# A five-layer attention kernel: key pieces moved from VectorE to GpSimd, three normalisations' scale and shift split between ScalarE and GpSimd, constants filled elsewhere, and a new order of steps

## The chip, the cores and the metric

The kernel runs on one core of a Trainium2 chip. A core has five engines, each working through its own instructions in order: TensorE (PE in the profile; its weight loads are PEld), VectorE (DVE), ScalarE (ACT), GpSimd (POOL) and SyncE (SP, which issues all DMAs here). They wait for one another by semaphores. The metric is the device time of one execution in microseconds.

## The reference

For each of 16 independent batch entries, x and a context of 256 tokens by 256 features go through five attention layers of 16 heads of 16 features each:

- `self` and `cross`: per head a 16 by 16 projection of keys, queries and values, masked softmax(QK/16), an output projection, a residual and a layer norm with gain and shift (ln1, ln2). `cross` is followed by a ReLU MLP of 1024 hidden features with its residual and norm (ln3).
- `l1`: a second norm of the queries (g_q, b_q), projections with bias, attention over the normalised context, output projection and residual.
- `l2`: windowed attention (64 tokens to either side) with a single key and value head, a gate (SiLU of a projection of the attention's output and the queries), an RMS norm, and the subtraction of the mean over tokens.
- `l3`: a norm, attention over the normalised context, residual, a norm, and a GELU MLP with its residual; its result is stored.

The keys of `self` and `cross` are the features of x and of the context themselves, since the key projection is folded into that of the queries.

## The kernel before, in words

**Work and stages.** Every batch entry is one chain of steps (CHAIN: some 40 steps for each layer) and one short chain beside it (BESIDE: loads, masks, the context's norm, the keys of the later layers). A tile has 128 partitions; 256 tokens or features are two such halves. Up to three batches are under way at once, each in its slot of buffers (SLOTS = 3).

**One attention layer on the engines.** `q` (PE, L1058 or L1293) projects. `ksplit` and `qsplit` cut keys and queries into three bfloat16 pieces each: the high piece by ScalarE (`high`, L697 to L712), the rest and the two lower pieces by VectorE (`low`, L841 to L866), then SP places them by six DMAs in a stack of 96 rows (L510), so that one bfloat16 matmul of 96 rows gives a nearly float32 product. `max0` to `max7` (PE L1096 and L1100, DVE L943) compute the scores of two heads each and their negated maxima. `pieces0`, `pieces1` (POOL, L664 and L667) cut the maxima of four such steps into three bfloat16 pieces, `turn0`, `turn1` (PE L1231, ACT L733, SP L523) turn them into three further rows of the query stack, against rows of ones in the key stack. `exp0` to `exp7` (PE L1118 to L1126, ACT L726) compute the scores again, less the maxima, and exponentiate; `weigh` (L1148 to L1157) multiplies by the values; `out`, `mix`, `outT` and `proj` normalise, turn and project. There are two score buffers and two `work` banks in PSUM.

**Norms.** `ln` (DVE, `moments`, L797 and L800) takes mean and variance, POOL makes the reciprocal root (L591 to L595), and `lnb` finishes on DVE. Where gain and shift are vectors (`self.ln`, `cross.ln`, `cross.ln3`, `cross.lnq`), it is done in two parts: `scale` (L816, subtract the mean, times the gain) while POOL works, and `shift` (L824, times the reciprocal root, plus the shift). `lnT` and `lnqT` transpose on PE (L1049), ScalarE takes the turned tile (`take`, L681), and POOL adds the next bias to the untransposed one for the next residual (`with_bias`, L605).

**Start.** VectorE fills values, PSUM and, at L787, rows 96 to 127 of the three key stacks with ones, and then lets PE, POOL and others go by the semaphore `zeroed`. Setup steps (`fold`, `columns_l1`, `row_l1` and so on) fold weights and biases once, among the first batches' steps.

**What sets the order.** Nothing is decided at run time. ORDER is a string of 3461 letters, written out by hand or by a program, each naming the chain whose next step comes: 0 to f the main chain of a batch, A to P the one beside it, s the setup. All engines walk through this one list, and each does its own part of every step; so ORDER, CHAIN, BESIDE and SETUP_STEPS fix the order of work in every queue, SP's too. Numbers count how often a semaphore must have been raised.

Of the kernel before, what the change touches and what calls it, by code (L numbers as in the profile page):

```python
# [8 lines left out]
ALU = mybir.AluOpType  # L9
# [31 lines left out]
     ("l3_b1", FC)],  # L41
# [26 lines left out]
for _name in BIAS_SOURCES:  # L68
# [19 lines left out]
    "self.mix0 self.values self.mix1 self.outT self.proj self.ln self.lnb self.lnT cross.q cross.qsplit cross.max0 "  # L88
# [3 lines left out]
    "cross.outT cross.proj cross.ln cross.lnb cross.lnT cross.hid1 cross.hid2 cross.hid3 cross.hid0 cross.hid_out "  # L92
# [22 lines left out]
def beside_steps():  # L115
# [7 lines left out]
ORDER = (  # L123
    "As0sAAsAAssA0001ssAssAA00A00sA2B00As01BB0B01B001s0000B000BA01B100001B10001010B0C11101C10C0C101B11110"
    "1C0011111221s100s01020000CsC00s100s0B2B10010s021221101C0C02s0021212200120002202022011022010212011100"
    "0012C110C001202C0211221AA10112001C21s112211001010200211102102011120010221000101D2211220222102100210B"
    "012B02200012D22122112C2C2002201122211021101111000212111112211202112111011012110020120120001211020012"
    "1022200110A210DA0011012101010021111D0101021212211021212121E200222002112212220202202BB202102012212200"
    "20200020202000110C0C000010221200s1001002002E0122220211202202002222222D1221010221121021101D1201321231"
    "1123322103112111112312312333131333312233133331313221D3DD3213D2E32D212E23321123E01242341322E2344E2EE3"  # L130
    "232232244E22E424423444F42E224D432444D43431424242444424E4332432334F3233F44332453343334433543343G342F3"
    "F343343344334F44443434F44454353DD4244F43444544F5F535354345355F545345555354534335543453453F5454555533"
    "4555345334353335F5435345E5344333343355E33353455353535554455355F55F5355355345434544354444534354454344"
    "4545543554433D5D4445444343343534335H34554333445435443534433354533E3544433E54454434434435544545535534"
    "43534544544443543534354435553345555G54554453553453443353353444443444445G34444444H3444444343443433345"
    "33343353335433345435345G54354443355G5355GG5353357566455565565555GG555565G665H666565466H676H576567366"
    "6656666H55677567777FH57F7776657H5777H7775G66H67767H77675I555777577755G755H375576575H57557675555556G5"
    "555577657777I57777766I57777H577I667H5776I75II655776I67I66I6766775876676676686676886I7675767766I76788"
    "666868686687768686778866878676886778G888688887678G678768677777768788J76778756767876867667867678777I8"
# [1300 lines left out]
```

## Time and profile before

| | us |
|---|---|
| median of 3 runs (lowest to highest) | 2636.02 (2631.29 to 2638.97) |
| profiled execution | 2635.18 |
| its span | 2633.4 |
| PE busy, 18862 matmuls | 2410.2 (92%) |
| DVE busy | 1590.7 (60%) |
| ACT busy | 1121.1 (43%) |
| POOL busy | 542.3 (21%) |

The span runs from the first to the last instruction; what lies around it is 1.8 us. Busy PE time is not PE at its peak: matmuls overlap, and the column of a group's mean is from a matmul's start to its modelled end. What a matmul really adds is seen where many follow one another in the chain of waits.

### The profile page before, as it was taken

How to read it: one execution, taken by the hardware profiler on the slowest of the kernel's cores; microseconds unless marked ns; L12 is line 12 of the kernel's file. 1: busy time of each engine (PE TensorE's matmuls, PEld its weight loads, DVE VectorE, ACT ScalarE, POOL GpSimd, SP SyncE). 2: the span in 40 equal slices, each digit the busy share in tenths (PEclk: the TensorE clock that was granted, in tenths of full speed). 3: DMA queues.
4: the chain of work that ended last, by engine and by line, in shares of the span. 5: the costliest groups of instructions: out<-in, count | busy, mean ns of one | idle time of the engine just before them, and what ended most of it. 6: DMA issues, size and time to landing. Idle time of an engine off the chain costs nothing.

```text
span 2633.4 us, 49701 instructions
## 1 busy us (share of the span) xinstructions
PE 2410.2 (92%) x18862; PEld 1749.2 (66%) x18862; DVE 1590.7 (60%) x2676; ACT 1121.1 (43%) x1762; POOL 542.3 (21%) x1278
## 2 busy tenths in 40 slices
PE   6999989999998898999989899999999999998976
PEld 4676766667676675766757567676767676676654
DVE  7756566665656557466574754766665757567432
ACT  1344345453444434535344344444444534544422
POOL 3221112222212132221112321111222212212110
PEclk8999999999999899999999999999999999999986
DMA  6412122231221122212111221211322221121100
GB/s 214 115 50 56 34 56 78 58 88 49 62 54 42 38 78 75 66 38 58 45 54 50 79 79 42 62 42 42 83 67 77 61 60 38 38 79 38 37 21 17
DMA packets 164235, 159.15 MB, mean 60 GB/s; under 512 B 17824, under 2 KB 162720, under 8 KB 162976
## 3 DMA queue, kind: packets, MB, share of 16 engines
q1 hardware_dynamic: 164000, 155.97, 21.6%
q8 instruction: 153, 2.51, 0.4%
q14 instruction: 82, 0.67, 0.1%
HBM read 35.71 MB, written 4.19 MB: 15 GB/s over the span
## 4 chain that ended last, share of the span: by engine, by line
PE 56%; issue 22%; DVE 8%; ACT 4%; POOL 3%; POOLq 2%; DVEq 2%; DMA 1%; SPq 1%; ACTq 0%
PE work L1067 13%; PE work L1058 11%; PE out L1148 6%; PE unit L1126 6%; PE unit L1100 5%; DVE neg_max L943 4%; PE unit L1096 4%; PE unit L1122 3%; ACT probs L726 2%; PE work L1049 2%; PE work L1263 2%; POOLq L669 1%; POOL resid L605 1%; DMA query_stack<-max_rows 1%; POOLq L666 1%
## 5 line engine op out<-in xcount | busy, mean ns | idle before, releaser
L943 DVE TENSOR_REDUCE neg_max<-unit 128x4 f32<-128x1024 f32 (+1 forms) x640 | 728.8, 1165 | 335.3 <-PE unit L1100 328.9
L726 ACT ACTIVATE probs<-unit 128x1024 f32<-128x1024 f32 (+1 forms) x640 | 609.1, 980 | 527.6 <-PE unit L1126 525.5
L1067 PE MATMUL work<-par,hidden_t 128*128 128x256 f32 x1792 | 417.9, 383 | 9.4 <-ACT hidden_t L681 6.0
L1100 PE MATMUL unit<-key_stack,query_stack 96*128 96x256 bf16 x2048 | 356.4, 280 | 35.4 <-DVE neg_max L943 17.9
L1067 PEld LDWEIGHTS work<-par,hidden_t 128*128 128x128 f32 x1792 | 332.4, 190 | 63.1 <-ACT hidden_t L681 9.7
L1126 PE MATMUL unit<-query_stack,key_stack 99*128 99x256 bf16 x2048 | 350.0, 277 | 25.6 <-ACT probs L726 9.2
L1058 PE MATMUL work<-tok_t,par 128*128 128x256 f32 x1408 | 339.0, 389 | 7.6 <-ACT tok_t L681 5.1
L1100 PEld LDWEIGHTS unit<-key_stack,query_stack 96*128 96x128 bf16 x2048 | 193.6, 100 | 162.4 <-DVE neg_max L943 38.6
L1058 PEld LDWEIGHTS work<-tok_t,par 128*128 128x128 f32 x1408 | 262.3, 194 | 49.6 <-ACT tok_t L681 9.9
L1148 PE MATMUL out<-probs,values 128*17 128x256 f32 x4096 | 269.6, 383 | 2.1 <-ACT probs L726 1.9
L1126 PEld LDWEIGHTS unit<-query_stack,key_stack 99*128 99x128 bf16 x2048 | 193.4, 99 | 90.0 <-ACT probs L726 19.4
L664 POOL CAST max_pieces<-neg_max 128x16 bf16<-128x16 f32 x160 | 34.0, 212 | 896.9 <-DVE neg_max L943 896.5
L757 ACT ACTIVATE hidden_t<-work,par 128x256 f32<-128x256 f32 x256 | 107.3, 470 | 191.3 <-PE work L1058 191.2
L1148 PEld LDWEIGHTS out<-probs,values 128*17 128x17 f32 x4096 | 95.6, 97 | 107.9 <-issue 48.3
L733 ACT CAST max_rows<-work 24x256 bf16<-24x256 f32 x160 | 57.0, 356 | 200.0 <-PE work L1231 199.6
L593 POOL TENSOR_SCALAR var_eps<-mv 128x2 f32<-128x2 f32 x112 | 25.4, 227 | 528.1 <-DVE mv L800 526.0
L681 ACT COPY tok_t<-work 128x512 f32<-128x512 f32 x96 | 56.1, 585 | 148.6 <-PE work L1049 148.2
L829 DVE TENSOR_TENSOR summed<-work,resid 128x512 f32<-128x512 f32 x64 | 44.2, 691 | 122.2 <-PE work L1067 121.9
L1263 PE MATMUL work<-ident,hidden_t 128*128 128x128 f32 x640 | 98.7, 282 | 15.6 <-ACT hidden_t L740 10.8
L1096 PE MATMUL unit<-neg_cross,ident_b 128*128 128x512 bf16 x256 | 97.6, 381 | 10.8 <-DVE neg_max L943 6.4
L963 DVE TENSOR_TENSOR hidden_t<-work,recip 128x256 f32<-128x256 f32 x160 | 99.5, 622 | 12.6 <-issue 0.9
L961 DVE RECIPROCAL recip<-work 128x16 f32<-128x16 f32 x160 | 40.0, 250 | 109.2 <-PE work L1263 108.6
(162 smaller groups left out, 3408.7 us busy)
## 6 DMA issues: line engine op xcount, KB each, us to landing
query_stack<-query_pieces SPq DMA_DIRECT2D x480, 128.0 KB, 2.4
key_stack<-key_pieces SPq DMA_DIRECT2D x384, 128.0 KB, 2.4
c_in<-in_ctx SPq DMA_DIRECT2D x16, 256.0 KB, 2.9
tok_t<-in_x_features SPq DMA_DIRECT2D x16, 256.0 KB, 2.8
ctx_t<-in_ctx_features SPq DMA_DIRECT2D x16, 256.0 KB, 3.0
x_in<-in_x SPq DMA_DIRECT2D x16, 256.0 KB, 3.1
m_in<-in_mask_self SPq DMA_DIRECT2D x16, 256.0 KB, 3.4
par<-in_params SPq DMA_DIRECT2D x4, 1024.0 KB, 6.3
```

Of the source, the lines that this page charges most:

```text
L726: a_.activation(probs[:, n % PROB_BUFS, :, :, 0:width(l)], bank[:, :, :, 0:width(l)], ACT.Exp, scale=SCALE[l]).then_inc(exped, 1)
L757: last = a_.activation(hidden_buffer(b, l)[:, f, :], bank[:, k, :], func, bias=pv(bias)[:, f:f + 1])
L943: v.tensor_reduce(neg_max[:, n % HALVES, :, 2 * (u % 4):2 * (u % 4) + 2], bank[:, :, :, 0:width(l)], AX.X, ALU.max, negate=True).then_inc( ...
L963: v.tensor_tensor(out_tok(b, l)[:, t, :].rearrange("p (c d h) -> p h c d", c=C, h=HC), slots[:, :, 0:HD].rearrange("p (h c) d -> p h c d", ...
L1058: last = pe.matmul(bank[:, k, :], pv(weight, C)[:, c, column + k * P:column + (k + 1) * P], src[:, c, :], start=(c == 0), stop=(c == C - 1))
L1067: last = pe.matmul(bank[:, t, :], src[:, t * P:(t + 1) * P], weight, start=(n == 0), stop=(n == len(parts) - 1))
L1096: pe.matmul(bank[:, t, :, 0:n], ident_b[:], twice(masked[:, t, 0:n], n), start=True, stop=False)
L1100: last = pe.matmul(bank[:, t, i, 0:n], queries[0:ROWS, h, t * P:(t + 1) * P], keys[0:ROWS, 0 if l == "l2" else h, columns(l, t)], start=ma ...
L1122: pe.matmul(bank[:, k, :, t * P:(t + 1) * P], masked[:, t, k * P:(k + 1) * P], twice(ident_b[:], P), start=(t == 0), stop=False)
L1126: last = pe.matmul(bank[:, k, i, 0:n], keys[0:MAX_ROWS, 0 if l == "l2" else h, k * P:(k + 1) * P], queries[0:MAX_ROWS, h, columns(l, k)], ...
L1148: last = pe.matmul(dst, values[b % SLOTS][:, k, head_in(NJ * g + j), :], p, start=(k == 0), stop=(k == T - 1))
L1263: last = pe.transpose(flatten(bank[:])[:, g * P:(g + 1) * P], out_t(b, l)[:, g, t * P:(t + 1) * P], ident[:])
```

## The change

Seven things change.

1. The low key pieces are made by POOL (`low_keys`). For `self` and `cross` POOL makes all of rest, second and third piece; for `l1`, `l2` and `l3` VectorE still makes the rest out of PSUM, which POOL can't read.
2. In `self.lnT`, `cross.lnT` and `cross.lnqT` VectorE gives the plain normalised tile (`layer_norm`); ScalarE puts gain and shift on the turned one, by one activation per half with a column of gains and one of shifts, and POOL multiplies the untransposed one by the gain. The shift is added once, at setup, to the bias that POOL adds anyway.
3. The ones of key stack 1 are written by ScalarE, of stacks 0 and 2 by POOL, with semaphores of their own, for which PE waits at the first `exp0` on each stack.
4. The third piece of the maxima is written by the subtraction itself, without a cast: four operations in place of five.
5. The hidden buffer of `self` and of `cross` comes free at another point (`wait_hidden_free`).
6. Six columns are added to the packed parameters.
7. CHAIN, BESIDE, SETUP_STEPS and ORDER are new. In `self`, `cross`, `l1` and `l3` `pieces0` follows four max steps, where it followed five in most layers before; the loads of batch 0 and 1 come first; `columns_l1` and `columns_l3` come later.

```diff
 BESIDE = (
-    "self.loadc self.loadct self.loadx self.loadm self.ctxln self.inputs self.loadm2 l2.keys l2.ksplit self.negc "
+    "self.loadc self.loadct self.loadx self.loadm self.inputs self.ctxln self.loadm2 l2.keys l2.ksplit self.negc "
 SETUP_STEPS = (
-    "par0 fold par5 par1 par7 wo_self wo_cross turn_wo columns_l1 par6 par4 columns_l3 par2 row_l1 row_l3 row_l2 "
-    "turn_bo par3 bg wg par8 "
+    "par1 par0 fold wo_cross wo_self par5 turn_wo par7 par8 par2 par6 par4 columns_l3 row_l2 columns_l1 par3 row_l1 "
+    "turn_bo bg wg row_l3 "
 ORDER = (
-    "As0sAAsAAssA0001ssAssAA00A00sA2B00As01BB0B01B001s0000B000BA01B100001B10001010B0C11101C10C0C101B11110"
+    "0AABAs1sAs000A1ABsAAs00s0A00000A00sBB0100B0s100BB0AB0s0B000110110001s10sA0sB01110B10112110A11100100s"
...
+            def ones_in_stack(n):
+                g.drain()
+                g.memset(key_stack[n][ROWS:P, :, :], 1.0).then_inc(stack_ones[n], 1)
+                g.drain()
+
+            ones_in_stack(0)
+            ones_in_stack(2)
             pool.wait_ge(setup_loaded, 48)
             pool.wait_ge(zeroed, 1)
...
+            def low_keys(key):
+
+                b, l, _ = key
+                part = (slice(0, HD), slice(0, 1)) if l == "l2" else (slice(0, P), slice(0, C))
+                piece = [key_pieces[part[0], n, part[1], :] for n in range(3)]
+                rest = key_rest[part[0], part[1], :]
+                if l in ("self", "cross"):
+                    pool.wait_ge(key_high, KSPLIT_NO.upto(key))
+                    g.tensor_tensor(rest, (tok_t[b % SLOTS] if l == "self" else ctx_t[b % CONTEXTS])[:], piece[0], ALU.subtract)
+                    g.drain()
+                else:
+                    wait_taken(pool, (b, l, "keys"))
+                g.tensor_copy(piece[1], rest).then_inc(key_low, 1)
+                g.drain()
+                g.tensor_tensor(piece[2], rest, piece[1], ALU.subtract).then_inc(key_low, 1)
...
+                    elif (l, step) in AFFINE:
+                        gain, _, bias = AFFINE[l, step]
                         wait_full_work(pool, key)
...
+                        g.tensor_tensor(resid[s][:], resid[s][:], row(gain), ALU.mult)
+                        g.drain()
+                        with_bias(resid[s], resid[s], bias)
...
-                        for piece in range(3):
-                            src = neg_max[:, half] if piece == 0 else max_rest[:]
-                            last = g.tensor_copy(max_pieces[:, n % HALVES, :, HC * piece:HC * (piece + 1)], src)
-                            if piece < 2:
-                                g.drain()
-                                g.tensor_tensor(max_rest[:], src, max_pieces[:, n % HALVES, :, HC * piece:HC * (piece + 1)],
-                                                ALU.subtract)
-                                g.drain()
-                        last.then_inc(max_cut, 1)
+                        piece = [max_pieces[:, n % HALVES, :, HC * k:HC * (k + 1)] for k in range(3)]
+                        g.tensor_copy(piece[0], neg_max[:, half])
+                        g.drain()
+                        g.tensor_tensor(max_rest[:], neg_max[:, half], piece[0], ALU.subtract)
+                        g.drain()
+                        g.tensor_copy(piece[1], max_rest[:])
+                        g.drain()
+                        g.tensor_tensor(piece[2], max_rest[:], piece[1], ALU.subtract).then_inc(max_cut, 1)
+                        g.drain()
...
         def _(act):
+            act.wait_ge(zeroed, 1)
+            a_.copy(key_stack[1][ROWS:P, :, :], ones[ROWS:P, 0:1].unsqueeze(2).broadcast_to((P - ROWS, H, S))).then_inc(stack_ones[1], 1)
...
-                    elif step in ("lnT", "lnqT"):
+                    elif (l, step) in AFFINE:
+                        gain, shift, _ = AFFINE[l, step]
+                        bank, taken = wait_full_work(act, key)
+                        wait_loaded(act, b, gain + "c", shift + "c")
+                        for c in range(C):
+                            last = a_.activation(tok_t[s][:, c, :], bank[:, c, :], ACT.Identity,
+                                                 scale=pv(gain + "c")[:, c:c + 1], bias=pv(shift + "c")[:, c:c + 1])
+                        last.then_inc(taken, 1)
+                    elif step == "lnT":
                         take(key, tok_t[s][:])
...
             v.memset(ones, 1.0)
-            for s in range(KEY_STACKS):
-                v.memset(key_stack[s][ROWS:P, :, :], 1.0)
...
-                        if l in ("self", "cross"):
-                            scale(scaled(b, l), summed[s], key)
-                    elif step == "lnb" and l in ("self", "cross"):
-                        shift(resid[s], scaled(b, l), (b, l, "ln"))
                     elif step == "lnb":
-                        layer_norm(norm[s], (resid if l == "l3" else summed)[s], (b, l, "ln"))
+                        layer_norm((resid if l in ("self", "cross") else norm)[s], (resid if l == "l3" else summed)[s],
+                                   (b, l, "ln"))
...
+                if u == 0 and l != "l2" and KEY_NO.place[b, l, "ksplit"] < KEY_STACKS:
+                    pe.wait_ge(stack_ones[KEY_NO.place[b, l, "ksplit"]], 1)
```

## Rows read from the trace of the kernel before

**Rows 1.** The page's first part: busy us, share, instructions of each engine.
```profile
PE 2410.2 (92%) x18862; PEld 1749.2 (66%) x18862; DVE 1590.7 (60%) x2676; ACT 1121.1 (43%) x1762; POOL 542.3 (21%) x1278
```

**Rows 2.** Busy time by stretch (count); then granted clock, DMA share, GB/s.
```profile
0.00:60.00 60.00, 38.18 (x182) 27.14 (x183) 44.87 (x78) 7.14 (x11) 19.25 (x37) 0.84 0.74 230
60.00:2500.00 2440.00, 2278.21 (x18118) 1657.04 (x18116) 1508.21 (x2533) 1079.51 (x1696) 510.72 (x1210) 0.99 0.22 59
2500.00:2634.00 134.00, 93.80 (x564) 65.06 (x564) 37.62 (x66) 34.40 (x57) 12.33 (x32) 0.80 0.07 19
```

**Rows 3.** Waits of TensorE, whole span: us in total, times, longest.
```profile
PE work L1168 <- DVEq L788: 19.0, 1, 19.0
PE unit L1100 <- DVE neg_max L943: 17.9, 32, 3.0
PE work L1231 <- POOL max_pieces L664: 17.8, 19, 2.5
```

**Rows 4.** The chain that ended last, in time: start, us, what.
```profile
70.24 0.22 PE unit L1126 x2
...
588.90 6.93 PE work L1067 x32
```

**Rows 5.** Timeline of the start: start, us, engine line operation.
```profile
4.29 0.20 POOL L583 MEMSET mean_w<- 128x128 f32 x1
...
6.78 3.47 DVE L787 MEMSET key_stack<- 32x4096 bf16 x1 [0.89 <-issue]
...
33.53 0.59 PE L1096 MATMUL unit<-neg_self,ident_b 128*128 128x512 bf16 x1
```

**Rows 6.** ScalarE, groups by form: busy us, mean ns, idle before.
```profile
L757 ACT ACTIVATE hidden_t<-work,par 128x256 f32<-128x256 f32 x256 | 107.3, 470 | 191.3 <-PE work L1058 191.2
...
L681 ACT COPY tok_t<-work 128x512 f32<-128x512 f32 x96 | 56.1, 585 | 148.6 <-PE work L1049 148.2
```

**Rows 7.** GpSimd, groups by form: busy us, mean ns, idle before.
```profile
L664 POOL CAST max_pieces<-max_rest 128x16 bf16<-128x16 f32 x320 | 73.0, 228 | 43.5 <-issue 2.4
L605 POOL TENSOR_TENSOR resid<-resid,par 128x512 f32<-128x512 f32 x48 | 56.3, 1172 | 128.1 <-PE work L1049 128.1
```

**Rows 8.** Timeline of the last batch's l3 attention, columns as in rows 5.
```profile
2564.52 3.78 PE L1058 MATMUL work<-tok_t,par 128*128 128x256 f32 x8 [0.68 <-ACT tok_t L681]
...
2569.31 3.81 SPq L510 DMA_DIRECT2D query_stack<-query_pieces  x6
...
2575.01 1.86 PE L1100 MATMUL unit<-key_stack,query_stack 96*128 96x256 bf16 x8 [6.71 <-issue]
...
2583.02 0.42 PE L1231 MATMUL work<-ident_b,max_pieces 128*128 128x128 bf16 x2
...
2586.10 1.03 PE L1126 MATMUL unit<-query_stack,key_stack 99*128 99x256 bf16 x4 [1.74 <-DMA query_stack<-max_rows]
```

**Rows 9.** VectorE by line (shortest/median/longest ns), then groups by form (busy us, mean ns).
```profile
L943 DVE TENSOR_REDUCE neg_max<-unit x640: 925/1215/1226, 35.7 to 2584.4; 128x4 f32<-128x1024 f32 x127, 128x4 f32<-128x768 f32 x33
...
L866 DVE TENSOR_TENSOR key_pieces<-key_rest,key_pieces x80: 411/693/1553, 23.1 to 2490.4; 128x512 bf16<-128x512 f32 x64, 16x256 bf16<-16x256 f32 x16
...
L864 DVE CAST key_pieces<-key_rest x80: 280/427/1543, 22.6 to 2489.9; 128x512 bf16<-128x512 f32 x64, 16x256 bf16<-16x256 f32 x16
...
L808 DVE TENSOR_SCALAR norm<-c_in,mv,rstd x32: 384/408/419, 40.6 to 2353.9; 128x256 f32<-128x256 f32 x32
...
L824 DVE SCALAR_TENSOR_TENSOR resid<-hidden_t,rstd,par 128x256 f32<-128x256 f32 x96 | 45.0, 510 | 5.3 <-POOL rstd L595 5.3
L816 DVE SCALAR_TENSOR_TENSOR hidden_t<-summed,mv,par 128x256 f32<-128x256 f32 x96 | 43.4, 493 | 4.4
```

**Rows 10.** Timeline at 841 us.
```profile
841.73 1.26 POOL L643 TENSOR_TENSOR hidden_t<-hidden_t,summed 128x512 f32<-128x512 f32 x1
...
841.80 1.66 DVE L808 TENSOR_SCALAR norm<-summed,mv,rstd 128x256 f32<-128x256 f32 x2 [2.14 <-POOL rstd L595]
```

**Rows 11.** Busy time of one stretch, columns as in rows 2.
```profile
865.00:880.00 15.00, 14.01 (x55) 7.94 (x54) 12.92 (x12) 1.31 (x3) 2.66 (x13) 0.50 0.12 36
```

More of the change, by code:

```diff
@@ L177 @@
 BIASES = (("self", "inputs"), ("self", "lnT"), ("cross", "lnT"), ("cross", "lnqT"), ("l2", "mean"), ("l3", "proj"))
-GAIN = {("self", "ln"): ("ln1_g", "ln1_b"), ("cross", "ln"): ("ln2_g", "ln2_b"), ("cross", "ln3"): ("ln3_g", "ln3_b"),
-        ("cross", "lnq"): ("g_q", "b_q")}
+AFFINE = {("self", "lnT"): ("ln1_g", "ln1_b", "bo_cross"), ("cross", "lnT"): ("ln2_g", "ln2_b", "l0_b2"),
+          ("cross", "lnqT"): ("g_q", "b_q", "bo_l1")}
 class Numbers:
@@ L361, in build @@
         zeroed = sem("zeroed")
+        stack_ones = [sem(f"stack_ones{s}") for s in range(KEY_STACKS)]
         band_ready = sem("band_ready")
@@ L433, in wait_hidden_free @@
             b, l = before
-            if l in ("self", "cross"):
-                act.wait_ge(normed, T * NORMED_NO.upto((b, l, "lnb" if l == "self" else "lnqb")))
-            elif l == "l1":
+            if l == "cross":
+                act.wait_ge(normed, T * NORMED_NO.upto((b, l, "ln3b")))
+            elif l in ("self", "l1"):
                 wait_full_work(act, (b, l, "proj"))
@@ L629, in run @@
                         negative(neg["cross"][s], 2 * b + 2)
+                    elif step == "ksplit":
+                        low_keys(key)
                     elif step == "values":
@@ L834, in low @@
                 of_keys = step == "ksplit"
-                pieces, done, ready, no = ((key_pieces, key_low, key_high, KSPLIT_NO) if of_keys
-                                           else (query_pieces, query_low, query_high, QSPLIT_NO))
-                rest = key_rest if of_keys else query_rest
+                if of_keys and l in ("self", "cross"):
+                    return
+                pieces, ready, no, rest = ((key_pieces, key_high, KSPLIT_NO, key_rest) if of_keys
+                                           else (query_pieces, query_high, QSPLIT_NO, query_rest))
@@ new lines, in low @@
+                bank, taken = wait_full_work(dve, (b, l, "keys" if of_keys else "q"))
+                if l in ("self", "cross"):
+                    last = v.tensor_tensor(rest[:], bank[:], pieces[:, 0], ALU.subtract)
+                elif of_keys and l == "l2":
+                    wait_loaded(dve, b, "bk_l2")
+                    v.tensor_copy(values_l2[b % SLOTS][:, :, 0:HD],
+                                  bank[:, 1, 0:T * HD].rearrange("p (t d) -> p t d", t=T))
+                    last = v.scalar_tensor_tensor(
+                        out=rest[0:HD, 0, :], in0=bank[0:HD, 0, :], scalar=pv("bk_l2")[0:HD, :],
+                        in1=pieces[0:HD, 0, 0, :], op0=ALU.add, op1=ALU.subtract)
+                else:
+                    wait_loaded(dve, b, "bk_" + l, "bq_" + l)
+                    bias = pv(("bk_" if of_keys else "bq_") + l)
+                    for c in range(C):
+                        last = v.scalar_tensor_tensor(
+                            out=rest[:, c, :], in0=bank[:, c, :], scalar=bias[:, c:c + 1],
+                            in1=pieces[:, 0, c, :], op0=ALU.add, op1=ALU.subtract)
@@ L862, in low @@
+                last.then_inc(taken, 1)
+                if of_keys:
+                    return
                 v.drain()
-                part = (slice(0, HD), slice(0, 1)) if of_keys and l == "l2" else (slice(0, P), slice(0, C))
-                v.tensor_copy(pieces[part[0], 1, part[1], :], rest[part[0], part[1], :]).then_inc(done, 1)
+                v.tensor_copy(query_pieces[:, 1], rest[:]).then_inc(query_low, 1)
                 v.drain()
-                v.tensor_tensor(pieces[part[0], 2, part[1], :], rest[part[0], part[1], :],
-                                pieces[part[0], 1, part[1], :], ALU.subtract).then_inc(done, 1)
+                v.tensor_tensor(query_pieces[:, 2], rest[:], query_pieces[:, 1], ALU.subtract).then_inc(query_low, 1)
@@ L917, in setup_step @@
                     last = v.tensor_tensor(pv(name), bank[:, 0, :], pv(name), ALU.add)
+                    if step == "row_l1":
+                        wait_loaded(dve, B, "b_q")
+                        v.drain()
+                        v.tensor_tensor(pv(name), pv("b_q"), pv(name), ALU.add)
                 elif step == "turn_bo":
@@ L994, in run @@
                         moments(norm[s], key)
-                        scale(scaled(b, l), norm[s], key)
                     elif step == "lnqb":
-                        shift(resid[s], scaled(b, l), (b, l, "lnq"))
+                        layer_norm(resid[s], norm[s], (b, l, "lnq"))
                     elif step == "hid_out":
```

116 lines of the change are left out of this document (50 added, 66 removed), and 33 rows, old and new, of the table CHAIN.

## The prediction

> **What bounds the kernel now.** I read the page first, then the busy time by stretch, the waits of TensorE, the groups of each other engine, and last the timeline of the start and the end. The page has TensorE (PE) busy for 92% of the span, VectorE (DVE) 60%, ScalarE (ACT) 43%, GpSimd (POOL) 21% [rows 1]. So no side engine is the bound on average; they matter where PE, which works through its list in order, has to wait for one. The three stretches of [rows 2] show where: PE idles 60.0 - 38.2 = 21.8 us in the first 60, 2440 - 2278.2 = 161.8 us in the 2440 of the middle (6.6%), and 134 - 93.8 = 40.2 us in the last 134, where only batches 14 and 15 are left and the clock is 0.80. Together 224 us. In the middle no single wait is long: the largest names are the maxima on DVE (17.9 us) and the pieces of maxima on POOL (17.8 us); the one long wait, 19.0 us, is the first matmul's [rows 3].
>
> How much could go at all? I weighed each step of ORDER by its TensorE time: 6.93/32 = 0.217 us for a float32 matmul of 256 columns, half of that for a bfloat16 one [rows 4], so 1.73 us for a projection, 6.93 for hid_out, 0.43 or 0.87 for a max or exp step without or with mask, 0.66 for l2's, 0.98 for a weigh. The steps are the same before and after and add up to about 2309 us. The span is 324 us above that: idle time, stretches at half clock, and waits too short to leave PE idle. That is the room.
>
> **The change, part by part.** The sum is made against the profiled execution's 2635.2 us (span 2633.4), 0.8 us under the median of the runs.
>
> *Start.* DVE fills three key stacks before it lets PE go: 3.47 us each with 0.8 between, so the first matmul is at 19.0 [rows 3]. Without them DVE is done at about 6.8, where the first of the fills began [rows 5]. ScalarE then makes one stack (a copy of 4096 elements a lane: at the 585 ns of its copies of 512 at most 4.7 us [rows 6], beside the loading of batch 0) and POOL two (no such row; DVE's 3.47 is the lower bound, and POOL's 228 ns for 16 elements and 1172 for 512 [rows 7] give 1.9 ns each, 7.8 us, the upper; I take 4, near DVE's row). But what PE needs for its first max is both stacks, and POOL now cuts the low key pieces after its two fills: its constants end at 4.5 [rows 5], so it is free at about 4.5 + 8 = 13 and done with three operations at 16.5. In the SP queue the six DMAs of the queries then take 3.8 us to issue, and at the end of the trace the first max follows 1.9 us behind the last of them [rows 8]. With the loads in the same queue that puts the first max near 23 to 25, not at 33.5 [rows 5]. That is 9 us earlier, but PE used the gap before for setup matmuls which now come later, in the dense part (some 3 us), and between the first maxima and the first exp there is then nothing to fill with. I take -6 (0 to -12). If POOL's fills took 7.8 each, the first max would be at 32 and the term 0.
>
> *DVE.* Gone are the key pieces, 64 x 0.427 + 16 x 0.28 = 32 us of casts and 64 x 0.693 + 16 x 0.41 = 51 of subtractions; the first subtraction in self and cross, 32 x 0.69 = 22; the fills, 10; `scale` of three norms (two thirds of 43.4, and 32 x 0.49 for lnq: 45) and the 45.0 us of `shift` into resid [rows 9]. Added: 96 plain normalisations at 0.41, 39 us. Net 32 + 51 + 22 + 10 + 45 + 45 - 39 = 166 us, so DVE falls to about 1425. What DVE has queued ahead of a maximum gets shorter by a tenth; of the waits of PE for it (17.9 us under the largest name alone [rows 3]) perhaps that share goes, and a little more where two waits meet: -5 (0 to -15).
>
> *POOL.* Added: 32 key splits of subtraction, cast, subtraction and 48 of the last two, 48 multiplications by the gain. A 512-element operation with two inputs is 1.17 us [rows 7]; a cast of 512 has no row, between 0.6 (half of that row) and 1.2; I take 0.8. So 32 x 3.2 + 32 x 2.0 + 16 x 1.1 + 48 x 1.17 + 8 for the fills = 248 us. One operation fewer in each of 160 pieces: -36 (0.228 x 160) [rows 7]. Net +212: 542 becomes about 750, 28%. The pieces of maxima now stand behind up to 3.2 us of a key split, and POOL, not DVE, waits for ScalarE's high piece and for DVE's rest. The cover is the PE work between the last max of a half and its turn (5.3 us on average in the new order, 6.0 in the old). Below nothing too: the pieces themselves end 0.35 us sooner, which stands in the counts below. I take +4 (0 to +25).
>
> *ScalarE.* Three transposes a batch are evicted by two activations of 470 ns instead of one copy of 585 [rows 6]: +0.36 us on the way lnT to q or hid, 48 times. Other batches' steps cover most; +3 (0 to +10).
>
> *New order.* Here I count, in PE work by the weights above, what ORDER places between a step and the one that needs it, and what falls short of the delay in between. The delays, from the end of the trace, where nothing else is in the way [rows 8]: q's end (2568.3) to first max 6.7 us; turn to exp 3.1; last maximum to turn: a reduction of 1.2 and five small POOL operations of 0.34 with their gaps, 2.9 (2.55 with four); exp to weigh 1.4, an estimate from ScalarE's 585 ns for half of its elements [rows 6]. Shortfalls, old to new order: turn to exp 30.3 to 19.1 us; q to max0 28.9 to 15.6; last max to turn 17.4 to 12.1; exp to weigh 10.1 to 2.8; four max steps in a row quicker than DVE's 1.22 each [rows 9], 21.4 to 11.8; gate to mean 12.5 to 7.6; the mix, outT, proj chain 51 to 50; proj to lnT 66 to 67; lnT to its reader 15.6 to 13. Sum 253 to 199. The middle's real idle time of 162 us is 0.64 of 253, and delays overlap once one has stalled; I take half of the difference of 54: -27 (0 to -50).
>
> *End.* The last batch's own chain (its l2 out to the store) is the same list with l3's keys put behind the rms, where PE has nothing of another batch; the small pieces come 0.35 us sooner in each half. -3 (+3 to -8).
>
> Sum: -6 - 5 + 4 + 3 - 27 - 3 = -34, so 2635.2 - 34 = 2601, and with the 0.8 us to the median 2602.
>
> **A row on the shared port.** At 841.73 a POOL subtraction of 1.26 us began, and DVE's pair of normalisations begun at 841.80 took 1.66 us in place of 2 x 0.41 [rows 10]; the longest key cast, 1.54 us against 0.43, is of the same kind [rows 9]. The trace so says that such an operation waits for POOL's to end. The Trainium skill (SBUF — State Buffer, "Who interferes with whom") states it as an exclusive lock that the later starter waits out, for copies, casts and tensor_scalar in a 2-port mode and for two SBUF inputs; it exempts the reduction. The trace agrees: no reduction is over 1.23 us [rows 9]. That speaks against moving work to POOL, and is the third rival.
>
> **Rivals.**
> 1. *POOL's queue takes PE's waits over (slower).* Place: the pieces of maxima behind low_keys and the gain multiplications. For: PE already loses 17.8 us to these pieces [rows 3], with POOL at 21%; in the new order there is 0.7 us less cover ahead of turn; and POOL, in order, now waits for ScalarE's high key piece and DVE's rest with the pieces behind it. Against: POOL stays at 28%. Price: 208 us of new work in operations of 1 to 3 us, a piece caught one time in three for 1.5 us is 0.5 x 160 = 80 us, half of it covered: +40. The other terms give -38, so it turns slower once the 160 pieces lose over 0.25 us each beyond cover; with a loss of 0.33 it is 2635 + 15 = 2650.
> 2. *The order's gain is not there (no change).* Stalls move from one kind to another, since each gap of PE is under 1 us; only start and end remain, and pay POOL and ScalarE: -9 - 5 + 7 = -7, so 2629 to 2636.
> 3. *DVE and POOL block each other (smaller gain).* About 160 new POOL operations of over 1 us that read two tensors. A meeting costs up to 1.54 - 0.43 = 1.1 us on the engine that comes second; if one in six meets, 27 x 1.1 = 30 us, a third of it on the path: +10, 2612. It is inside the forecast's range.
> 4. *More falls than counted.* For 15 us the clock is at 0.50, 1.2 GHz, behind a stretch in which PE waited for DVE [rows 11]. The middle's mean of 0.99 [rows 2] means some 2% of 2440 us at that level, 49 us in which 24 are lost. If the better spacing clears them all, 24 us more: 2578.
>
> That the code does something else than it says I exclude: each part can be followed in the diff.
>
> **Chances.** Forecast (2580 to 2622, rival 3 in it) 0.58; rival 4 0.12; a gain of under 14 but over 8 us 0.04; rival 2 within 0.3% (2628 to 2644, about what a measurement can tell here) 0.11; rival 1 over that 0.15. So faster 0.74, same 0.11, slower 0.15. The range takes in rival 4 and the no-change case: 2568 to 2645; the forecast's own is 2580 to 2622.
>
> **What would show it.** The first matmul at 6 to 8 us and the first max at 23 to 25 (start); DVE busy about 1420, POOL about 750, ACT about 1140; PE's idle time in the middle falling from 162 to about 130, with the waits on max_rows and neg_max down most (order); the wait of the turn for POOL's pieces staying near 18 us (if it is over 40, rival 1 has it); casts and normalisations with tails of 1.2 to 1.6 us more often (rival 3); a mean clock above 0.975 (rival 4). Wrong in mechanism if PE's idle time in the middle does not fall.

## The result, and the profile after

The kernel after takes 2496.24 us (median of 4 runs, 2493.62 to 2500.58), the kernel before 2636.66 (median of 4): a ratio of 0.947, 95% interval 0.9453 to 0.9486. The change is worth 140 us. Forecast were 34 us, with a range of 2568 to 2645: the direction was right, the size was four times too small, and the time lies 72 us below the range. The profiled execution has a span of 2493.4 us and a mean granted clock of 0.981 (before 0.975).

The page after, first part: busy us, share, instructions of each engine, to be held against [rows 1].

```profile
PE 2371.6 (95%) x18862; PEld 1748.3 (70%) x18862; DVE 1427.9 (57%) x2388; ACT 1138.9 (46%) x1809; POOL 732.3 (29%) x1360
```

The three side engines are where they were forecast: DVE 1427.9 (some 1425), ACT 1138.9 (1140), POOL 732.3 (750). What the moved work costs them was counted rightly; what it was worth to TensorE was not. Busy time by stretch of the kernel after, columns as in [rows 2] (the middle is cut at 2360, so that the last 134 us stand alone):

```profile
0.00:60.00 60.00, 42.69 (x263) 24.33 (x264) 31.73 (x56) 17.77 (x21) 34.00 (x52) 0.97 0.82 258
60.00:2360.00 2300.00, 2233.69 (x18025) 1657.08 (x18025) 1355.86 (x2264) 1085.93 (x1730) 685.06 (x1279) 0.99 0.22 61
2360.00:2494.00 134.00, 95.24 (x577) 66.87 (x575) 40.33 (x69) 35.24 (x58) 13.27 (x30) 0.82 0.08 23
```

PE idles 60.0 - 42.7 = 17.3 us at the start (21.8 before [rows 2]), 66.3 in the middle (161.8) and 38.8 at the end (40.2). The middle carries nearly all of it. The idle time falls by 101 us in all; the other 39 us of the span are PE's own busy time (2410.2 to 2371.6), of which the clock explains at most about 18: 2633.4 x (1 - 0.975) = 65.8 us of full-speed work lost before, 2493.4 x (1 - 0.981) = 47.4 after. By the same working in the rows of the stretches some 8 of these 18 lie in the first 60 us (clock 0.84 before, 0.97 after) and some 3 in the last 134 (0.80 and 0.82).

Waits of PE after, over the whole span: us in total, times, longest. Of before, [rows 3] answer.

```profile
PE work L1088 <- DVE norm L846: 9.8, 5, 3.7
PE unit L1139 <- issue: 9.1, 4, 6.8
PE unit L1139 <- DVE neg_max L986: 7.6, 15, 1.6
PE work L1272 <- POOL max_pieces L698: 7.5, 14, 0.9
...
PE work L1209 <- DVEq L826: 6.1, 1, 6.1
PE work L1213 <- DMA par<-in_params: 5.2, 1, 5.2
...
PE unit L1135 <- DVE neg_max L986: 4.1, 11, 0.6
```

The wait for a score buffer that DVE has to empty fell from 17.9 to 7.6 us, the one for GpSimd's pieces from 17.8 to 7.5 although GpSimd works 190 us more, and the start's 19.0 to 6.1; one new wait of 5.2 us, for the parameters' DMA, took a part of that over. One name is only one of several lines that wait for the same thing: added over all of them, PE waits 42.9 us for maxima before and 15.5 after.

The gain has no place of its own. At the moments when the same amount of TensorE work has been done (steps weighed as in the prediction, 2309 us in all), the kernels stand at 580 and 540 us (500 us of work), 1254 and 1174 (1100), 2130 and 2003 (1900), 2620 and 2480 (2300): 5 to 7% at each of them.

### The profile page after: what moved, and what is told of

Read it like the earlier page. It is cut to its first block, busy times and chain, and to the rows that moved or that the text cites. A ratio compares the mean times of both kernels' runs of the same rounds, so it can differ in the third digit from the quotient of the medians.

```text
span 2493.4 us, 49454 instructions
## 1 busy us (share of the span) xinstructions
PE 2371.6 (95%) x18862; PEld 1748.3 (70%) x18862; DVE 1427.9 (57%) x2388; ACT 1138.9 (46%) x1809; POOL 732.3 (29%) x1360
## 4 chain that ended last, share of the span: by engine, by line
PE 49%; issue 29%; POOL 7%; POOLq 6%; DVE 5%; ACT 2%; DVEq 1%; DMA 1%; SPq 1%; ACTq 0%
PE work L1106 11%; PE work L1097 9%; PE unit L1167 6%; PE out L1189 5%; PE unit L1139 5%; PE unit L1135 3%; DVE neg_max L986 3%; PE unit L1163 2%; PE work L1088 2%; POOL resid L630 2%; POOL rstd L604 2%; POOL key_pieces L627 1%; PE work L1304 1%; POOLq L668 1%; PE unit L1159 1%
## 5 line engine op out<-in xcount | busy, mean ns | idle before, releaser
L602 POOL TENSOR_SCALAR var_eps<-mv 128x2 f32<-128x2 f32 x112 | 26.2, 234 | 367.3 <-DVE mv L838 363.2
L1135 PE MATMUL unit<-neg_self,ident_b 128*128 128x512 bf16 x256 | 100.3, 392 | 4.3 <-DMA query_stack<-query_pieces 2.5
L1163 PE MATMUL unit<-ident_b,neg_self 128*128 128x256 bf16 x512 | 98.8, 274 | 1.6 <-DMA query_stack<-max_rows 0.7
L892 DVE SCALAR_TENSOR_TENSOR query_rest<-work,par,query_pieces 128x256 f32<-128x256 f32 x96 | 41.9, 477 | 101.7 <-ACT query_pieces L744 101.4
```

What stands on the lines that cost most here:

```text
L1135: pe.matmul(bank[:, t, :, 0:n], ident_b[:], twice(masked[:, t, 0:n], n), start=True, stop=False)
L1163: pe.matmul(bank[:, k, :, t * P:(t + 1) * P], masked[:, t, k * P:(k + 1) * P], twice(ident_b[:], P), start=(t == 0), stop=False)
```

## The experiments

Two questions: is it the order or the moved work, and by what mechanism? Ratios are against the kernel before on the same chip, with 95% intervals. A difference between two ratios is known to some 4 to 6 us.

### The order alone, and everything but the order

e2 is the kernel before with the four strings of the new order; e1 is the kernel after with the old ones.

```diff
 # e2_only_order: before.py; BESIDE, SETUP_STEPS and ORDER likewise
-    "self.loadxt self.ksplit self.q self.qsplit self.max0 self.max2 self.max1 self.max3 self.max4 self.pieces0 "
...
+    "self.loadxt self.ksplit self.q self.qsplit self.max0 self.max3 self.max2 self.max1 self.pieces0 self.max4 "
...
```

> The kernel before with the four new strings and nothing else. Theory O: 2500 to 2535 us. Theory D: 2600 to 2640, PE's waits for VectorE as before. Theory T: over 2640, because the new order packs VectorE's steps for a load that is a tenth smaller.

> The changed kernel with the four strings of before (CHAIN, BESIDE, SETUP_STEPS, ORDER). Theory O, the new order carries the gain: little is left, 2615 to 2635 us (the start's fills alone give some 10). Theory D, the work taken off VectorE carries it and any order would do: 2510 to 2540. Theory T, the two only work together: 2600 or slower than before, since the old order places the key splits where POOL is needed for maxima.

Measured: e2 2575.30 us, 0.977 (0.9755 to 0.9786): the order alone gives 61 us. e1 2638.78, 1.0019 (1.0007 to 1.0031): all the moved work without the order gives nothing, or loses 5. So 140 is not a sum of two independent terms: the order gives 61 alone and 142 on top of the moved work, the moved work 79 on top of the order and nothing alone. e1 falls to Theory T. e2 lies between Theory O and Theory D and fits neither.

Busy time of the middle, from 60 us to the last 135, columns as above: before, e1, e2.

```profile
60.00:2499.00 2439.00, 2277.62 (x18115) 1656.69 (x18114) 1507.52 (x2532) 1079.14 (x1695) 510.72 (x1210) 0.99 0.22 59
```

```profile
60.00:2507.00 2447.00, 2271.29 (x18068) 1651.98 (x18067) 1372.39 (x2250) 1094.35 (x1738) 686.54 (x1287) 0.99 0.21 58
```

```profile
60.00:2441.00 2381.00, 2262.32 (x18104) 1667.37 (x18102) 1498.13 (x2544) 1070.90 (x1684) 513.76 (x1209) 0.98 0.22 61
```

Before, DVE is busy for 1508 us and PE idles for 161. e1 has DVE at 1372 and lets PE idle for 176; e2 has it at 1498 and lets it idle for 119. A less busy DVE is by itself worth nothing here. The waits of PE, e1, then e2:

```profile
PE unit L1139 <- DVE neg_max L986: 18.8, 30, 3.5
PE work L1272 <- POOL max_pieces L698: 15.6, 14, 3.4
PE unit L1135 <- DVE neg_max L986: 12.8, 32, 1.1
PE work L1304 <- ACT hidden_t L772: 11.5, 17, 1.2
```

```profile
PE work L1231 <- POOL max_pieces L664: 22.7, 35, 2.5
...
PE unit L1100 <- DVE neg_max L943: 10.9, 20, 1.7
PE unit L1096 <- DVE neg_max L943: 10.7, 23, 1.5
```

e1's first two rows are close to those of before ([rows 3]: 17.9 and 17.8). With a tenth less work DVE still holds PE up for 18.8 us at a score buffer. What goes down where is seen when PE's waits are added over all lines by what they wait for (us; e3, the kernel after with the keys on DVE, follows below):

| PE waits for | before | e1 | e2 | e3 | after |
|---|---|---|---|---|---|
| DVE, maxima (`neg_max`) | 42.9 | 43.8 | 38.0 | 32.0 | 15.5 |
| POOL, pieces of maxima | 17.8 | 15.6 | 22.7 | 9.7 | 7.5 |
| DVE, `resid` | 4.9 | 4.3 | 12.8 | 6.4 | 1.5 |
| ACT, `probs` | 24.4 | 26.2 | 8.8 | 9.0 | 8.5 |
| ACT, `hidden_t` | 19.6 | 20.3 | 8.0 | 8.0 | 8.0 |
| ACT, `tok_t` | 6.2 | 15.9 | 2.5 | 6.7 | 6.4 |
| DMA of `max_rows` | 13.2 | 17.0 | 6.2 | 6.2 | 7.3 |
| all waits over 0.15 us | 211.6 | 223.0 | 174.6 | 146.8 | 111.4 |

The order alone takes away waits for ScalarE (`probs` and `hidden_t`, 44 to 17 us) and for the rows' DMA, and hardly any for maxima. Those fall when work leaves DVE, but only in the new order: 38.0 to 15.5 there, 42.9 to 43.8 in the old one.

### Which moved work, in the new order

Each kernel is the one after with one part undone.

```diff
 # e3_keys_on_dve: VectorE cuts the low key pieces again
-                    elif step == "ksplit":
-                        low_keys(key)
...
-                if of_keys and l in ("self", "cross"):
-                    return
...
+                if of_keys and l in ("self", "cross"):
+                    v.tensor_tensor(rest[:], (tok_t[b % SLOTS] if l == "self" else ctx_t[b % CONTEXTS])[:], pieces[:, 0],
+                                    ALU.subtract)
```

> The changed kernel with the low key pieces made by VectorE again (about 100 us more of VectorE, 170 less of POOL), order as changed. Theory O: within 15 us of 2496. Theory D: VectorE's load sets the time in proportion, 100 of 166 us returned, so 0.6 of the 140 us is lost, about 2580.

Measured: 2543.30 us, 0.9658 (0.9637 to 0.9678): the keys carry 47 us (50 by the ratios), more than Theory O allows and less than Theory D. The timeline of that kernel at 588 us shows how: start, us, what, idle time before it.

```profile
587.90 0.38 PE L1140 MATMUL unit<-neg_self,ident_b 128*128 128x512 bf16 x1
588.12 0.38 PE L1144 MATMUL unit<-key_stack,query_stack 96*128 96x256 bf16 x2
588.19 1.36 DVE L903 CAST key_pieces<-key_rest 128x512 bf16<-128x512 f32 x1
588.34 1.89 PE L1102 MATMUL work<-tok_t,par 128*128 128x256 f32 x8
589.64 0.69 DVE L905 TENSOR_TENSOR key_pieces<-key_rest,key_pieces 128x512 bf16<-128x512 f32 x1
590.25 2.35 DVE L991 TENSOR_REDUCE neg_max<-unit 128x4 f32<-128x1024 f32 x2
...
591.62 0.38 PE L1168 MATMUL unit<-ident_b,neg_cross 128*128 128x256 bf16 x2 [1.38 <-DVE neg_max L991]
```

Both score buffers are full at 588.5. DVE has a key cast and a subtraction ahead of their reductions in its list, begins the first at 590.25, and PE, which ran out of other work at 590.24, stands for 1.38 us. Added up over all 640 reductions, DVE's busy time with writing key pieces between the end of a max step's last matmul and the start of its reduction is 17 us before, 40 in e2, 39 in e3 and 0 after. In the new order the key pieces stand more than twice as long ahead of a full buffer, and 39 us is near the 47 that moving them brings. It is not a price, though: in the old order the same count falls from 18 (e6 below) to 0 (e1), and that brings nothing.

```diff
 # e4_norms_on_dve: scale and shift of three normalisations on VectorE again
-                        g.tensor_tensor(resid[s][:], resid[s][:], row(gain), ALU.mult)
-                        g.drain()
...
-                            last = a_.activation(tok_t[s][:, c, :], bank[:, c, :], ACT.Identity,
-                                                 scale=pv(gain + "c")[:, c:c + 1], bias=pv(shift + "c")[:, c:c + 1])
 # e8_fills_on_dve: VectorE fills the key stacks before it lets PE go
+            for s in range(KEY_STACKS):
+                v.memset(key_stack[s][ROWS:P, :, :], 1.0).then_inc(stack_ones[s], 1)
 # e5_pieces_old: the third piece of the maxima by a subtraction and a cast again
-                        g.tensor_tensor(piece[2], max_rest[:], piece[1], ALU.subtract).then_inc(max_cut, 1)
```

> The changed kernel with gain and shift of the three normalisations on VectorE again (about 51 us more of VectorE, 56 less of POOL, 17 less of ScalarE), order as changed. Theory O: within 10 us of 2496. Theory D: 0.3 of the 140 us lost, about 2540.

> The changed kernel with all three key stacks filled by VectorE ahead of the semaphore that lets TensorE go, as before. Price of the fills by my step: 6 us, so 2502. If TensorE's first gap is bound by the parameters' loads or by the key pieces instead: within 2 us of 2496. If VectorE's 12 us go straight into the start: 2508.

> The changed kernel with the maxima pieces in five GpSimd operations as before: 0.35 us more on each of 160 ways from the last maximum to its turn. If one in four of them is on the path: 14 us more, 2510. If it is covered: within 3 us of 2496.

Measured: e4 2503.38 us, 0.9501 (0.9486 to 0.9517), 7 us; e8 2503.48, 0.9509 (0.9492 to 0.9526), 7; e5 2507.13, 0.9502 (0.9486 to 0.9519), 11. The 7 of e4 and e8 are little more than the ratios can tell. With the keys' 47 that is 72, and with the order's 61 it is 133 of the 140; the other 7 lie within what the ratios leave open. In e5 the turn's wait is the one that grew, from 7.5 us to

```profile
PE work L1272 <- POOL max_pieces L693: 18.2, 28, 1.5
```

One operation of a quarter of a microsecond in each of 160 pieces was worth the 11 us, near the 14 expected: two thirds of 160 x 0.23 = 37 are covered, a third is not.

### Which moved work, in the old order

e6 is e1 with e3's edit, e7 is e1 with e4's.

```diff
 # e6_old_order_keys_dve: e1_old_order and e3's edit
-                        low_keys(key)
 # e7_old_order_norms_dve: e1_old_order and e4's edit
-                        g.tensor_tensor(resid[s][:], resid[s][:], row(gain), ALU.mult)
```

> The changed kernel with the old order and the low key pieces on VectorE: only norms, fills and the short maxima pieces differ from before. Theory L (in the old order VectorE's load is simply not on PE's path): 2625 to 2637, the start's 3 us at most. Theory P (moving the keys to GpSimd gains on VectorE in the old order too and loses it again in GpSimd's queue): this one, without the keys, is clearly faster than the 2639 of the old order with all parts, 2610 to 2625.

> The changed kernel with the old order and the norms on VectorE: keys on GpSimd, fills and short maxima pieces stay. Theory L: 2632 to 2642, as with all parts. Theory P: 2640 to 2650, since the keys on GpSimd cost in that order, whatever the norms do.

Measured: e6 2637.98 us, 1.0009 (0.9998 to 1.002); e7 2625.46, 0.9968 (0.9955 to 0.998). So in the old order moving the keys brings nothing (3 us the other way, the intervals overlap), where in the new one it saves 47; moving the normalisations costs 13 where it saves 7. The prices of one and the same edit differ by 50 and by 20 us with the order around them. e6 is as Theory L had it, 1 us over its upper edge; e7 lies below both of its theories: they had not asked what the normalisations cost on ScalarE. The waits of PE show a part of it. For the turned tile (`tok_t`), which ScalarE now makes by two activations, PE waits 15.9 us in e1 and 7.7 in e7, and the rows of the new form are, in e1:

```profile
PE work L1334 <- ACT tok_t L780: 5.1, 7, 2.0
PE work L1097 <- ACT tok_t L780: 4.9, 12, 1.1
```

In the new order the same two rows are 2.4 and 1.2 us.

### Is it the spacing that I had counted?

The prediction priced the order by spacing: how much TensorE work stands between a step and the one that needs it. One rule it had only for four max steps in a row: with two score buffers every max or exp step must stand some time behind the step two before it, 1.35 us behind a max and 1.15 behind an exp. (These are estimates: in e3's timeline above PE starts at 591.62, 1.37 us after the reduction that frees its buffer began at 590.25.) By that rule the old order falls short by 121 us and the new one by 60, a difference that coincides with e2's 61. To test it I moved steps in the kernel before until one count was down and the others stood.

```diff
 # e9_spaced_units: before.py, max and exp steps moved in the whole order: buffers 121 to 68, other gaps 239
 # e10_other_gaps: before.py, max and exp steps moved in the whole order: other gaps 237 to 195, buffers 122
-    "As0sAAsAAssA0001ssAssAA00A00sA2B00As01BB0B01B001s0000B000BA01B100001B10001010B0C11101C10C0C101B11110"
...
 # e11_pe_units: before.py, TensorE's list alone moved, the other engines' kept: buffers 121 to 84
-    "1C0011111221s100s01020000CsC00s100s0B2B10010s021221101C0C02s0021212200120002202022011022010212011100"
+    "1C0011111221s100s0102000Cs0C00s100s0B2B10010s021221101C0C02s0021212200120002202022011020120212011100"
...
 # e12_pe_others: the same way, other gaps 237 to 195
 # e13_after_pe_all: after.py, the same way, buffers 60 to 49, other gaps 195 to 166
```

> The kernel before, nothing changed but ORDER, in which max and exp steps alone are moved by a few places. Each such step fills one of two PSUM score buffers and must wait until VectorE or ScalarE has emptied it two steps earlier; what ORDER's PE work falls short of 1.35 us (max) and 1.15 us (exp) there adds up to 121 us in the old order, 60 in the new, 68 in this one; the sum of all other shortfalls is as in the old order (239 against 237). Theory U, these two buffers carry the new order's gain: 53 us less in the count and about as much in time, 2575 to 2595. Theory G, the other gaps carry it (projections, turns, norms): 2620 to 2640.

> The opposite: the kernel before with max and exp steps moved so that the other shortfalls fall from 237 to 195 us, as in the new order, and those of the two score buffers stay at 122. Theory U: 2620 to 2640. Theory G: 2580 to 2600.

> The kernel before, nothing changed but ORDER, in which TensorE's steps alone are moved by a few places and only past steps with which they share no other engine, score buffer or work bank: every other engine runs its old sequence. The score-buffer shortfall of the count falls from 121 to 84 us, that of the other gaps stays at 237. If the count is a fair price of TensorE's spacing once the other engines' sequences are kept: 2595 to 2615 us. If the count prices nothing (the two earlier reorderings, which also moved steps in the other engines' sequences, cost 137 and 161 us): 2630 or slower.

> The same kind of moves, with the other gaps' shortfall down from 237 to 195 us and that of the score buffers kept at 120. If the count is a fair price: 2590 to 2615 us, as the other. If only the score buffers matter: 2625 to 2637. If the count prices nothing: 2630 or slower.

> The changed kernel with the same kind of moves, both shortfalls down, 60 to 49 and 195 to 166 us. If the count is a fair price: 2455 to 2480 us, faster than both kernels. If it prices nothing: 2496 or slower.

Measured: e9 2771.50 us, 1.0513 (1.0495 to 1.0531); e10 2795.21, 1.0621 (1.0604 to 1.0638); e11 2645.46, 1.0048 (1.0032 to 1.0064); e12 2656.74, 1.0082 (1.0064 to 1.01); e13 2526.39, 0.9596 (0.9576 to 0.9615), 30 us slower than the kernel after. Each of these five lists has a smaller count than the one it was made from and is slower; e9 and e10 lie far outside both of their theories, e11 to e13 where the theory had them by which the count prices nothing. A max or exp step that is moved to widen one gap moves in VectorE's or ScalarE's list too (e9, e10; GpSimd's and the DMA queues' lists are as before there). In e11 to e13 only PE's list changed; that it then no longer agrees with the others is my reading of the loss. e9's waits of PE show where it comes back:

```profile
PE work L1231 <- POOL max_pieces L664: 31.0, 28, 3.5
PE unit L1100 <- DVE neg_max L943: 27.9, 38, 3.7
PE unit L1096 <- DVE neg_max L943: 20.5, 28, 2.6
```

The buffers that it spaced out on paper are waited for longer (17.9 to 27.9 us; over all lines that wait for maxima 42.9 to 73.8). In e11 the waits for maxima do fall, 42.9 to 35.5, but those for the DMA of `max_rows` rise from 13.2 to 20.5 and all together from 211.6 to 216.3. The count is refuted as a price, mine of the prediction and the one with the missed rule.

### Is it where GpSimd cuts the maxima?

From the last of a half's four maxima to the start of its pieces, GpSimd lets 0.73 us pass before and 0.34 in e2 (mean of 160); in the kernel before 15 of the late pieces stand behind a reciprocal root that waits for DVE. So the order's gain might be these lists' and no more.

```diff
 # e14_pieces_at_once (before.py), e15_after_pieces_at_once (after.py), for GpSimd's list alone
+        at = max(keys.index(key[:2] + (f"max{4 * a + n}",)) for n in range(4))
+        keys.insert(at + 1, key)
 # e16_after_pieces_fifth (after.py): pieces0 behind the fifth max step, as the old order has it
+        fifth = sorted(keys.index(key[:2] + (f"max{n}",)) for n in range(8))[4]
```

> The kernel before; after the old schedule is unrolled, each pieces0 and pieces1 is moved to directly behind the last of its four maxima. Only GpSimd takes part in these steps, so every other engine keeps its old sequence, and 41 of 160 have another GpSimd step ahead of them. Theory Q, GpSimd's sequence (a reciprocal root that waits for VectorE's moments, or a bias, standing ahead of pieces that are ready) was a large part of what the new order mended: 26 pieces start over 0.8 us late there, 106 us in total, 13 in the new order, 44 us; half on the path gives 2595 to 2615 us. If GpSimd's lateness was covered all along: 2628 to 2640.

> The same move in the changed kernel (28 pieces get another GpSimd step ahead). Theory Q: 21 late pieces, 62 us in total are left there, so 2475 to 2492, faster than both kernels. Otherwise 2493 to 2500.

> The changed kernel with pieces0 moved, for GpSimd alone, from behind the fourth max step to behind the fifth, as in most layers of the old order (22 get another GpSimd step ahead). Theory Q: 2505 to 2520. Otherwise 2493 to 2500.

Measured: e14 2635.92 us, 0.9995 (0.9985 to 1.0005); e15 2512.23, 0.9525 (0.9509 to 0.9541); e16 2527.06, 0.9585 (0.9565 to 0.9606). e14 did what it was to do: the mean lateness fell from 0.73 to 0.12 us, the pieces over 0.8 us late from 26 to 2. It is worth nothing in the old order, so it is not the order's gain. In the new one 16 us go when they are cut at once, though they then start 0.13 us behind the maxima in place of 0.45, and 31 when they are cut one step later; neither of Theory Q and its opposite had that. e16's wait at the turn is then

```profile
PE work L1285 <- POOL max_pieces L711: 28.7, 23, 4.5
```

against 7.5 us after. The added lateness in e16 is 160 x (0.73 - 0.45) = 45 us, and 31 are paid. In e15 the turn's wait is 7.8 us, so its 16 us lie elsewhere, with the steps of GpSimd that now come behind the pieces; which of them is not shown. It is a pattern like that of the key pieces: what a side engine's microsecond costs depends on the order around it, 98 us of lateness less being worth nothing in the old order and 45 more costing 31 in the new one.

## Why the prediction was wrong, by its own steps

**Start (-6): right in its mechanism, near in its size.** The timeline of the kernel after:

```profile
4.63 3.51 POOL L588 MEMSET key_stack<- 32x4096 bf16 x1
...
5.95 3.60 ACT L709 CAST key_stack<-summed 32x4096 bf16<-32x4096 f32 x1 [3.95 <-DVEq L826]
6.06 1.20 PE L1209 MATMUL work<-norm 128*128 128x128 f32 x4 [6.06 <-DVEq L826]
...
23.11 0.59 PE L1135 MATMUL unit<-neg_self,ident_b 128*128 128x512 bf16 x1 [0.33 <-DMA key_stack<-key_pieces]
```

The first matmul came at 6.06 us (6 to 8 forecast), the first max at 23.11 (23 to 25); GpSimd's fill took 3.51 us, at DVE's row of 3.47 and far from the bound of 7.8, and ScalarE's 3.60. e8, in which the first matmul waits 19.0 us again, prices the fills at 7 us.

**GpSimd's and ScalarE's work: right.** For ScalarE's longer way (+3) e4 agrees in the new order: PE's waits for `tok_t` are 6.4 us after and 2.9 in e4. In the old order it costs more, 15.9 against 7.7 (e1, e7). GpSimd by form: busy us, mean ns, idle before.

```profile
L627 POOL TENSOR_TENSOR key_pieces<-key_rest,key_pieces 128x512 bf16<-128x512 f32 x64 | 74.6, 1166 | 10.3 <-issue 10.0 <-PE work L1106 0.2 <-PE work L1304 0.2
L667 POOL TENSOR_TENSOR resid<-resid,par 128x512 f32<-128x512 f32 x48 | 58.5, 1218 | 54.2 <-PE work L1088 53.8 <-issue 0.3
...
L625 POOL CAST key_pieces<-key_rest 128x512 bf16<-128x512 f32 x64 | 40.7, 637 | 83.4 <-DVE key_rest L892 78.5
```

The subtraction took 1.17 us, as taken from [rows 7]; the cast 0.64, at the lower bound (0.6) and not at the 0.8 chosen. The same subtraction is 0.69 us on DVE [rows 9]. The Trainium skill (GPSIMD Engine Reference, "3.1 Elementwise — side-by-side cycle accounting") says of such operations that "use DVE for elementwise" stays the rule, since GpSimd takes longer, about twice as long in its table. The trace agrees on the duration (1.17 against 0.69 us), and the runs contradict the rule for this kernel: in the new order the slower engine was worth 47 us (e3), and in the old one it made no difference (e6).

**The DVE term (-5, bounds 0 to -15): the first step that failed.** I took DVE's relief, a tenth of its work, as a tenth of one wait. In the old order that was even too much (e1: no gain). In the new one the keys alone gave 47, three times the bound of 15, and the normalisations 7. The mistake was to price the term with the waits of the old order while another term of the sum changed the order: the terms don't add. The question to put was where in DVE's list of the *new* order the key pieces stand against full score buffers: 40 us (e2), against 17 in the old. It would have pointed to the keys; it would not have given the price, since the 17 were worth nothing.

**The order term (-27, bounds 0 to -50): failed in size and in its basis.** e2 measures -61, outside the bounds. Of the waits that were to fall most, that for the rows' DMA did (13.2 to 6.2 us in e2) and that for maxima hardly (42.9 to 38.0); most went from the waits for ScalarE. The count had the mix, outT, proj chain as unchanged (51 to 50), where the waits for `hidden_t` fell from 19.6 to 8.0, and it had no term for a score buffer that ScalarE has to empty (most of `probs`, 24.4 to 8.8). The count of shortfalls had the two score buffers only in part; made anew with them it reads 237 + 121 to 195 + 60, a difference of 103 in place of 54. But e9 to e13 show that such a count is no price: five lists with a smaller count ran slower. It looks at PE's list, and each of the other lists is in order too.

**GpSimd (+4) and rival 1 (its queue takes over, 2650): refuted.** The turn's wait is 7.5 us, where 18 were to stay and 40 would have spoken for the rival. The rival's mechanism is real, though, at the margin: e5 and e16 give 11 and 31 us for a quarter of a microsecond and for one step's delay. That the shorter pieces save 11 us by themselves was put at 3 at the end and otherwise left in the counts.

**Rival 2 (order's gain not there): refuted** by e2. **Rival 3 (blocking, +10): too large.** Casts, low subtractions and plain normalisations of DVE exceed their undisturbed 427, 693 and 408 ns by 18 us in all after (mean minus that, times count, by form) and by 13 before: 5 us more, where 30 were put. The longest did occur as forecast (a subtraction of 1.68 us), only seldom. **Rival 4 (clock): true in a small part.** It had the 24 us of the middle cleared. The clock gave at most 18 us in all, but some 8 of them at the start and 3 at the end, so about 7 in the middle, whose clock reads 0.99 before and after. And e2 has its 61 us at a clock of 0.973, below that of before, so the clock did not cause the order's gain.

**The end (-3): about right**: 38.8 us idle against 40.2. In sum the failed steps are the two that asked what the change gives PE in the middle, where 32 us of idle time less were forecast (162 to 130) and some 96 were measured.

**Left open.** What in the new order gives the 61 us is not settled. They show as less idle time of PE ahead of max and exp steps: 60 us ahead of max and 40 ahead of exp before, 43 and 27 in e2, 32 and 16 after; and, by what PE waits for, above all as shorter waits for ScalarE (table above). No list that I changed by itself gives any of it in the old order (PE's in e11 and e12, GpSimd's in e14), but these lists were of my making and not those of the new order, and no run changed VectorE's, ScalarE's or the DMA queue's list alone. PE's or GpSimd's list moved away from the new order loses 16 to 31 us (e13, e15, e16). That all five lists fit each other is what remains; it is argued, not shown. A kernel with only the new order of steps within a batch, or only the new mixing of batches, would divide it further; none was run.

## What to carry to other kernels

Where several engines work through lists in order, the value of taking work off an engine that isn't the bound depends on the order around it: the same edit was worth nothing in one order and 47 us in another. The time between "buffer full" and "its reader starts" that such work fills, read in the order that the changed kernel will have, shows where to look (40 us there, 17 in the old order), but it is no price. When order and placement change together, don't add terms priced on the old trace; and don't price an order by counting gaps in one engine's list, since the five lists that were made better by that count ran slower.

## What the hardware showed that I had not expected

GpSimd's fill of 32 x 4096 bfloat16 ones took 3.51 us, DVE's 3.47 [rows 5]: for a fill GpSimd is no slower than VectorE here, where for a subtraction of 512 elements it is by 1.17 to 0.69. ScalarE's copy of 4096 float32 from one broadcast element took 3.60 us, 0.88 ns an element, against 585 ns for 512, 1.14 ns.
